# Attention over 16 heads: score tiles issued in groups of three halves instead of four, the value products behind each group, and the work at both ends of the attention reordered

## The chip, the core and the metric

The kernel is one launch on one core of a Trainium2 chip. The core has five engines with in-order instruction queues: TensorE (PE in the profile, its weight loads PEld), VectorE (DVE), ScalarE (ACT), GpSimd (POOL) and SyncE (SP, here only a DMA queue). The metric is the device time of the launch in microseconds; the median of repeated runs is given. SBUF is the on-chip working memory, PSUM the eight banks (128 partitions by 512 fp32 each) that TensorE writes.

## What is computed

The input x has 2 images of 128 channels by 32 by 32 pixels (n = 1024 positions). Each of two blocks normalises x in groups of 4 channels, computes something and adds it to x.

```
x = x + attention(groupnorm(x))        # 8 heads of 16 channels, per image
    q, k, v = W[head] @ t + bias       # (16 x 16) weights per head
    attn = softmax((q^T k) * 16**-0.5, axis=-1)    # 1024 x 1024 per head
    out  = Wp[head] @ (attn @ v) + bp
x = x + convnext(groupnorm(x))         # depthwise 7x7 conv, layernorm over channels,
    h = gelu(y @ w1 + b1)              # 128 -> 512
    y = h @ w2 + b2                    # 512 -> 128
```

There are T = 16 heads in all, heads 0 to 7 for image 0 and 8 to 15 for image 1.

## The kernel before

**Tiles.** A head has NT = 8 tiles of 128 keys; n counts the tiles of all heads (0 to 127). A tile's transposed scores are 128 keys by 1024 queries, made as two halves of 512 columns (`scores_t`, L1040), each in one PSUM bank. h = 2n + c counts these halves. ScalarE takes exp of each half into `pr`, a ring of PR = 4 tiles (L654). `times_v` (L1051) multiplies a whole tile with the values, in four matmuls of 32 output columns, each of which is two instructions. It accumulates a head in one bank.

**The maximum first.** The softmax needs the maximum of each query. For this, the scores are also computed untransposed (`scores`, L993; 2 halves of 512 into one of the two pairs of banks in `sm`) and reduced by VectorE (`maxima`, L766, 128 x 1024), AHEAD = 13 tiles earlier than the exp. `scores(k, 0)` must wait until the maximum of tile k-2 is done, because it reuses its banks. The 8 maxima of a head are split in two parts by GpSimd, turned by TensorE (`turn_max`, L1025), copied by ScalarE (L619) and sent by SP into two more rows of `qs`, so that `scores_t` subtracts them.

**Order of a head.** TensorE's queue is written out by hand: `both_scores(n)` issues for each half one `scores_t` and one `scores` of tile n+13. The two read different 64-row parts of `qs` and `ks` except in the first three tiles of an even head, and can then run side by side. After every second tile come `times_v(n-2)` and `times_v(n-1)`: so the order is four halves, then two value products. The halves, one "turn" use per head (transposed maxima and transposed results, after tile 4) and six "finish" uses (heads 8 and 9 end the attention of image 0; head 14 holds the two group-norm products "mean" and "var" of block 2) take the three banks 4, 5, 7 in rotation. A use waits until the use three before it has been read.

**Before the heads.** TensorE projects q and k of image 0 (L943), runs matmuls on zeros that only keep it active (`keep_busy`, L969), and starts `scores(0)` when the split rows of q and k have been stacked into `qs` and `ks` by DMA (`stack`, L357; SP for q, ScalarE's queue for k). Between the first 13 `scores` tiles stand the value projection of image 0 (`project_v`, L954), both projections of image 1 and its value projection.

**Behind the heads.** In heads 14 and 15 TensorE also runs 56 shifted conv matmuls (L1145, 4 to a unit, 112 instructions) and VectorE twelve conv taps of image 0; then the layernorm of image 0 (`centre_out` L1169, `ln_var`, `ln_turn`, `ln_scale` L1196), the transposes and the projection that end the attention of image 1 (L1240, L1246), the MLP (L1210, L1224), and the same for image 1, whose conv starts after its padded input has been refilled by 32 DMAs (L379).

## Time and profile before

| | us |
|---|---|
| three runs | 312.48, 319.83, 409.74 |
| median of them | 319.83 |
| profiled execution, whole | 313.76 |
| profiled execution, span of the trace | 312.0 |

The execution lasts 1.76 us longer than the span that the trace covers. Within the span PE is busy for 94%, DVE 73%, ACT 57%, POOL 26%. In the page's 40 slices the heads lie in slices 5 to 32. The granted TensorE clock is full but for slice 31, from 234 to 242 us. A busy PE in the page says little, since the ends of matmuls are modelled and overlap: what counts is the distance between the starts of groups, and which wait stands before them. Columns of a timeline row: start, duration, engine, line, operation, output and inputs with their shapes, count of merged instructions, and in brackets the idle time of the engine before and what ended it.

### The profile page before, as it was taken

The page shows a single profiled execution, that of the slowest core. Times are in us where ns is not written, and L with a number is a line of the kernel's source. Part 1 is how long each engine was busy: PE and PEld are TensorE (multiplying, and loading weights), DVE is VectorE, ACT ScalarE, POOL GpSimd, SP SyncE. Part 2 cuts the span into 40 slices and gives each one's busy share as a digit, 9 for nine tenths or more (in the row PEclk, how much of TensorE's full clock was granted, in tenths as well). Part 3 has the DMA queues.
Part 4 walks back from the last instruction along what each step waited for, and adds up shares of the span by engine and source line. Part 5 has one row for each costly group of instructions (what it writes and reads, how often), then busy time and mean ns, then how long its engine had stood idle before and what let it go on. Part 6 is the DMA issues. An engine that isn't in the chain of part 4 may idle for free.

```text
span 312.0 us, 5509 instructions
## 1 busy us (share of the span) xinstructions
PE 291.8 (94%) x2123; PEld 133.2 (43%) x2125; DVE 228.8 (73%) x264; ACT 176.5 (57%) x354; POOL 79.7 (26%) x103
## 2 busy tenths in 40 slices
PE   7999999999999999999999999999989779899895
PEld 2453544454454454454454454444323334323342
DVE  2838868888889979887678989989970228986421
ACT  1304468778778878777778777763173724011321
POOL 7100624323000000000018789983200200101010
PEclk9999999999999999999999999999996999999999
DMA  6275003213203203202113398000000004650001
GB/s 218 36 125 119 1 0 55 35 20 54 43 8 54 47 11 53 52 14 39 29 25 69 103 195 174 8 3 1 2 0 0 2 0 100 159 170 0 2 34 34
DMA packets 8489, 16.32 MB, mean 52 GB/s; under 512 B 2564, under 2 KB 3716, under 8 KB 8464
## 3 DMA queue, kind: packets, MB, share of 16 engines
q1 hardware_dynamic: 7888, 14.96, 22.4%
q10 hardware_dynamic: 576, 1.02, 1.6%
q8 instruction: 17, 0.28, 0.4%
q14 instruction: 8, 0.07, 0.1%
HBM read 4.96 MB, written 1.73 MB: 21 GB/s over the span
## 4 chain that ended last, share of the span: by engine, by line
PE 76%; ACT 8%; DVE 8%; SPq 3%; issue 2%; DMA 2%; POOL 0%; DVEq 0%; ACTq 0%; POOLq 0%
PE ps L1040 19%; PE ps L1051 19%; PE ps L1145 10%; ACT pr L654 7%; PE ps L993 7%; DVE mx L766 4%; PE ps L1210 3%; PE ps L969 3%; SPq L379 3%; PE ps L943 3%; PE ps L1224 2%; PE ps L1169 2%; PE ps L1030 2%; DVE ot L776 2%; PE ps L954 1%
## 5 line engine op out<-in xcount | busy, mean ns | idle before, releaser
L766 DVE TENSOR_REDUCE mx<-ps 128x1 f32<-128x1024 f32 x128 | 151.2, 1220 | 32.9 <-PE ps L993 32.7
L654 ACT ACTIVATE pr<-ps 128x512 f32<-128x512 f32 x256 | 133.2, 602 | 52.9 <-PE ps L1040 52.5
L1040 PE MATMUL ps<-qs,ks 50*128 50x512 f32 x256 | 96.7, 445 | 7.8 <-ACT pr L654 4.9
L993 PE MATMUL ps<-ks,qs 48*128 48x512 f32 x256 | 97.7, 444 | 0.7 <-DVE mx L766 0.7
L1051 PE MATMUL ps<-pr,va 128*32 128x256 f32 x1024 | 69.2, 387 | 0.4 <-ACT pr L654 0.4
L1040 PEld LDWEIGHTS ps<-qs,ks 50*128 50x128 f32 x256 | 43.2, 186 | 61.3 <-ACT pr L654 41.2
L993 PEld LDWEIGHTS ps<-ks,qs 48*128 48x128 f32 x256 | 42.6, 184 | 10.7 <-DVE mx L766 3.5
L1051 PEld LDWEIGHTS ps<-pr,va 128*32 128x32 f32 x1024 | 26.6, 109 | 29.5 <-ACT pr L654 11.5
L804 DVE SCALAR_TENSOR_TENSOR hl<-xpad,w,hl 128x512 f32<-128x512 f32 (+1 forms) x37 | 35.6, 962 | 0.9
L479 POOL CAST mparts<-mx 128x8 fp32r<-128x8 f32 x16 | 3.1, 191 | 127.8 <-DVE mx L766 127.8
L1145 PE MATMUL ps<-xr,wt 128*32 128x512 f32 x272 | 31.1, 594 | 1.0 <-DMA xr<-xpad 1.0
L566 POOL TENSOR_TENSOR hl<-hl 128x1024 f32<-128x1024 f32 x11 | 26.5, 2408 | 0.9
L1210 PE MATMUL ps<-yc,w1g 128*128 128x512 f32 x32 | 15.6, 608 | 2.5 <-DVE yc L848 2.5
L969 PE MATMUL ps<-warm 128*128 128x512 bf16 x57 | 15.7, 409 | 1.6 <-POOL warm L462 1.4
L570 POOL TENSOR_TENSOR rstd<-vareps,power 128x4 f32<-128x4 f32 (+1 forms) x3 | 4.1, 1375 | 47.6 <-DVE vareps L831 47.6
L1145 PEld LDWEIGHTS ps<-xr,wt 128*32 128x32 f32 x272 | 8.0, 109 | 19.0 <-issue 15.9
L711 ACT ACTIVATE pr<-ps,b1s 128x512 f32<-128x512 f32 x8 | 5.5, 688 | 16.8 <-PE ps L1210 16.8
L348 POOL TENSOR_TENSOR gn_rstd<-gn_vareps,power 128x1 f32<-128x1 f32 x4 | 3.8, 942 | 38.1 <-DVE gn_vareps L320 38.1
L563 POOL TENSOR_SCALAR hl<-xpad,w 128x1024 f32<-128x1024 f32 x11 | 12.5, 1140 | 0.7
L609 ACT ACTIVATE va<-ps 128x128 f32<-128x128 f32 x16 | 2.9, 304 | 13.3 <-PE ps L954 13.3
L687 ACT ACTIVATE diag<-inside,w,nshift 128x1024 f32<-128x1024 f32 x2 | 2.5, 1237 | 13.3 <-issue 13.3
L1210 PEld LDWEIGHTS ps<-yc,w1g 128*128 128x128 f32 x32 | 5.6, 189 | 10.1 <-issue 4.7
(104 smaller groups left out, 211.2 us busy)
## 6 DMA issues: line engine op xcount, KB each, us to landing
qs<-hl SPq DMA_DIRECT2D x48, 64.0 KB, 2.4
ks<-hl SPq DMA_DIRECT2D x42, 64.0 KB, 2.4
xr<-xpad SPq DMA_DIRECT2D x16, 95.0 KB, 2.2
xr<-pad_dram SPq DMA_DIRECT2D x4, 361.0 KB, 6.4
xr<-pad_dram SPq DMA_DIRECT2D x4, 304.0 KB, 5.4
xr<-xpad SPq DMA_DIRECT2D x8, 76.0 KB, 2.1
xr<-xpad ACTq DMA_DIRECT2D x8, 76.0 KB, 2.2
xs<-x SPq DMA_DIRECT2D x2, 256.0 KB, 3.0
```

The source lines that it names most:

```text
L379: queue.dma_start(xr[s * CG:(s + 1) * CG, g, lo:hi], xpad[g * CG:(g + 1) * CG, lo + s:hi + s])\
L563: nc.gpsimd.tensor_scalar(image(product), window(0, tap), weight(tap), 0.0, ALU.mult, ALU.add)\
L566: nc.gpsimd.tensor_tensor(acc_pool, acc_pool, product, ALU.add).then_inc(S("pool_tap"), 1)
L654: nc.scalar.activation(pr[:, n % PR, c * HALF:(c + 1) * HALF], bank("half", n, c), ACT.Exp, scale=SCALE).then_inc(exp_done, 1)
L766: nc.vector.tensor_reduce(mx[:, s % 2, i:i + 1], sm[(NT * s + i) % 2], AX.X, ALU.max).then_inc(max_done, 1)
L804: nc.vector.scalar_tensor_tensor(out=sums, in0=window(k, tap), scalar=weight(tap), in1=sums, op0=ALU.mult, op1=ALU.add).then_inc(S("dve_ta ...
L969: nc.tensor.matmul(pv, warm[:, 0:P], warm[:, :], start=True, stop=True)
L993: last = nc.tensor.matmul(sm[k % 2][:, c * HALF:(c + 1) * HALF], qs[rows, cell_of(s) + i * P:cell_of(s) + (i + 1) * P], ks[rows, cell_of(s ...
L1040: nc.tensor.matmul(bank("half", n, c), ks[rows, cell_of(t) + j * P:cell_of(t) + (j + 1) * P], qs[rows, cell_of(t) + c * HALF:cell_of(t) + ...
L1051: last = nc.tensor.matmul(out_v[q * VW:(q + 1) * VW, :], va[:, n * VW:(n + 1) * VW], pr[:, n % PR, 2 * P * q:2 * P * (q + 1)], start=(j == ...
L1145: last = nc.tensor.matmul(conv_out[g * CG:(g + 1) * CG, half * HALF:(half + 1) * HALF], wt[:, g * KS * SPAN + m, :], rows[:, :, 0:SIDE], s ...
L1210: last = nc.tensor.matmul(sm[f % 2][:, cols], w1g[:, f * P:(f + 1) * P], yn[:, b, cols], start=True, stop=True)
```

## The change

- **Groups of three.** `BURST = 3`: TensorE issues three halves, then the value products (`times_v_after`): one when the group ended in the middle of a tile, two when it ended with a tile (and other numbers where a head's first tile is put off, so that it needn't wait for the copy of the head before). The turn and the six finish uses are moved to ends of such groups (`burst_end`).
- **Consequences in other queues.** ScalarE copies a head's result (`copy_u`) after half 3 or 4 of the next head instead of half 1, and makes the conv's border term (`border(0)`) after half 13 of head 14 instead of half 1 of head 15. VectorE normalises a head one tile later.
- **Ahead of the heads.** The value projection of image 0 and one projection of image 1 go in front of `scores(0)`, in the place of 27 keep-busy matmuls (4 are left). The bias product of the MLP (`first_bias`, 4 matmuls) and its addition on VectorE go from head 14 and the end of the conv into the 13 tiles ahead. The stacks of heads 0 and 1 go to SP but for one DMA, and the MLP's weights are loaded before the stacks of heads 2 and 3.
- **Behind the heads.** The transposes and projection of image 1's attention go before the MLP of image 0 (they stood inside it); `turn_u(15)` goes before `ln_scale(0)`, which no longer waits for ScalarE's copy; the other uses of `ln_scale` wait for the product before.

```diff
-TURN_AT = 4
+BURST = 3
 BANKS = (4, 5, 7)
-FINISH = {(HEADS, 6): ("oc", 0), (HEADS + 1, 0): ("oc", 1), (HEADS + 1, 2): ("proj", 0), (HEADS + 1, 6): ("proj", 1),
-          (T - 2, 4): ("mean",), (T - 2, 6): ("var",)}
+
+
+def burst_end(t, x):
+
+    h = 2 * NT * t + x
+    return h + (BURST - 1 - h) % BURST
+
+
+def turn_at(t):
+
+    return burst_end(t, NT)
+
+
+FINISH = {burst_end(HEADS, 13): ("oc", 0), burst_end(HEADS + 1, 1): ("oc", 1), burst_end(HEADS + 1, 5): ("proj", 0),
+          burst_end(HEADS + 1, 13): ("proj", 1), burst_end(T - 2, 10): ("mean",), burst_end(T - 2, 13): ("var",)}
...
             sp.dma_start(bv[:, :], bvrow.rearrange("a p -> p a")).then_inc(S("bv"), 16)
             for n in range(PARTS):
                 stack(sp, 0, 0, n)
-            sp.wait_ge(S("part11", 0), 2)
-            for n in range(PARTS):
-                stack(sp, 0, 1, n)
+            stack(sp, 1, 0, 0, (2,))
+            stack(sp, 1, 0, 1)
+            for i in range(2):
+                for n in range(PARTS):
+                    stack(sp, i, 1, n)
+            sp.dma_start(w1s[:, :], w1).then_inc(S("w12"), 16)
+            sp.dma_start(w2s[:, :, :], w2.rearrange("(f p) c -> p f c", p=P)).then_inc(S("w12"), 16)
             sp.wait_ge(S("minus"), 1)
...
+                for h in range(2 * NT * t, 2 * NT * (t + 1)):
+                    n, c = divmod(h, 2)
+                    a.wait_ge(st_ready, h + 1)
+                    if c == 0 and n >= PR:
+                        a.wait_ge(pv_done, n - PR + 1)
+                    nc.scalar.activation(pr[:, n % PR, c * HALF:(c + 1) * HALF], bank("half", n, c), ACT.Exp,
+                                         scale=SCALE).then_inc(exp_done, 1)
+                    if t and h == 2 * NT * t + (3 if t % BURST else 4):
                         copy_u(t - 1)
-                    if j == TURN_AT and t + 1 < T:
+                    if h == turn_at(t) and t + 1 < T:
                         copy_max(t + 1)
                         if t:
                             copy_turned(t - 1)
...
+            also[2 * NT * (T - 2) + 13] = lambda: border(0)
+            also[2 * NT * (T - 1) + 9] = lambda: ln_square(0)
...
-            keep_busy(9)
+            project_v(0, 0, NT)
+            value_bias()
+            project(1, 0)
...
+            def times_v_after(h):
+
+                n = h // 2
+                if h % 2 == 0:
+                    if n >= PR and (n - PR) % NT == 0:
+                        times_v(n - 4)
+                    if n >= BURST:
+                        times_v(n - 3)
+                else:
+                    if n >= BURST:
+                        times_v(n - 3)
+                    if (n - 2) % NT:
+                        times_v(n - 2)
+
+            def head(t, also=()):
+
+
+                for h in range(2 * NT * t, 2 * NT * (t + 1)):
+                    n, c = divmod(h, 2)
                     scores_t(n, c)
                     if n + AHEAD < NT * T:
                         scores(n + AHEAD, c)
-
-            def head(t, also=()):
-
-
-                for j in range(NT):
-                    n = NT * t + j
-                    both_scores(n)
-                    if j == TURN_AT:
+                    if h % BURST == BURST - 1:
+                        times_v_after(h)
+                    if h == turn_at(t):
                         free("turn", t)
                         if t:
                             turn_u(t - 1)
                         if t + 1 < T:
                             turn_max(t + 1)
-                    if n < 2:
...
-            value_bias()
-            keep_busy(18)
+            keep_busy(4, sm[0][:, 0:HALF])
             for k in range(AHEAD):
                 for c in range(2):
                     scores(k, c)
-                if k == 0:
-                    keep_busy(2)
-                if k in (1, 2):
-                    project_v(0, 4 * (k - 1), 4 * k)
-                if k in (3, 4):
-                    project(1, 0, k - 3, k - 2)
-                if k in (6, 7):
-                    project(1, 1, k - 6, k - 5)
-                if k == NT:
+                if k in (1, 3):
+                    project(1, 1, k // 2, k // 2 + 1)
+                if k == 4:
                     t_.wait_ge(S("copied0"), 1)
-                if k in (NT, NT + 1, NT + 4):
-                    keep_busy(2)
-                if k == NT + 1:
+                if k == 5:
+                    first_bias()
+                if k in (7, 9):
+                    project_v(1, 2 * (k - 7), 2 * (k - 5))
+                if k == 9:
+                    t_.wait_ge(S("b1"), 1)
                     turn_max(0)
-                if k in (NT + 2, NT + 3):
-                    project_v(1, 4 * (k - NT - 2), 4 * (k - NT - 1))
+                if k in (4, 6, 8, 10, 11, 12):
+                    keep_busy(1 + k // 10)
...
             def ln_scale(k):
                 t_.wait_ge(S("diag"), k + 1)
-                t_.wait_ge(*((S("yn"), 2) if k == 2 else (S("yc"), k + 1)))
+                if k:
+                    t_.wait_ge(S("yn"), k)
...
-            head(T - 2, [(5, first_bias)] + [(3 + n * 5 // (2 * units), *quads[n]) for n in range(2 * units)])
+            head(T - 2, [(3 + n * 5 // (2 * units), *quads[n]) for n in range(2 * units)])
             head(T - 1, [(3, centre_out, 0), (5, ln_var, 0), (6, ln_turn, 0)])
-            times_v(NT * T - 2)
-            times_v(NT * T - 1)
+            for n in range(NT * T - 3, NT * T):
+                times_v(n)
+            turn_u(T - 1)
             ln_scale(0)
-            turn_u(T - 1)
-            mlp(0, 0)
             t_.wait_ge(ot_done, T)
             for i in range(NT):
                 last = nc.tensor.transpose(lower[:, i * P:(i + 1) * P], ot[:, i, P:2 * P], ident)
                 if i % (NT // 2) == NT // 2 - 1:
                     last.then_inc(S("ot_T", 1), 1)
-            mlp(0, 1, 0)
             for c, done in enumerate((S("oc", 1), S("oc_low"))):
                 t_.wait_ge(done, 1)
                 nc.tensor.matmul(lower[:, c * HALF:(c + 1) * HALF], vec(C_WP, P), oc[:, 1, c * HALF:(c + 1) * HALF],
                                  start=True, stop=True).then_inc(S("projp", 1), 1)
-            mlp(0, 1, 1)
-            mlp(0, 2)
-            mlp(0, 3)
+            for f in range(FC):
+                mlp(0, f)
```

TensorE in the middle of the heads, before: L1040 is `scores_t`, L993 `scores`, L1051 the value products (four matmuls a tile, so x8 is two tiles).

```order
L1051 MATMUL ps<-pr,va 32x256 x8
L1040 MATMUL ps<-qs,ks 128x512
L993 MATMUL ps<-ks,qs 128x512
L1040 MATMUL ps<-qs,ks 128x512
L993 MATMUL ps<-ks,qs 128x512
L1040 MATMUL ps<-qs,ks 128x512
L993 MATMUL ps<-ks,qs 128x512
L1040 MATMUL ps<-qs,ks 128x512
L993 MATMUL ps<-ks,qs 128x512
L1051 MATMUL ps<-pr,va 32x256 x8
```

The same place of the changed kernel, where the three lines are L1070, L1023 and L1081.

```order
L1081 MATMUL ps<-pr,va 32x256 x8
L1070 MATMUL ps<-qs,ks 128x512
L1023 MATMUL ps<-ks,qs 128x512
L1070 MATMUL ps<-qs,ks 128x512
L1023 MATMUL ps<-ks,qs 128x512
L1070 MATMUL ps<-qs,ks 128x512
L1023 MATMUL ps<-ks,qs 128x512
L1081 MATMUL ps<-pr,va 32x256 x4
```

Six rows of scores instead of eight stand between two groups of value products, which alternate between one tile and two.

TensorE ahead of the heads, before: L969 are the keep-busy matmuls, L963 is `value_bias`, L954 `project_v`, L943 a projection.

```order
L342 MATMUL ps<-gn_spread,w 128x1
L969 MATMUL ps<-warm 128x512 x9
L963 MATMUL ps<-bv,w 128x1
L969 MATMUL ps<-warm 128x512 x18
L993 MATMUL ps<-ks,qs 128x512 x2
L969 MATMUL ps<-warm 128x512 x2
L993 MATMUL ps<-ks,qs 128x512 x2
L954 MATMUL ps<-w,xn 128x128 x4
L993 MATMUL ps<-ks,qs 128x512 x2
L954 MATMUL ps<-w,xn 128x128 x4
```

And in the changed kernel (L975 `project_v`, L964 a projection, L997 keep-busy, L991 `first_bias`).

```order
L975 MATMUL ps<-w,xn 128x128 x8
L984 MATMUL ps<-bv,w 128x1
L964 MATMUL ps<-xn,w 128x512 x2
L997 MATMUL ps<-warm 128x512 x4
L1023 MATMUL ps<-ks,qs 128x512 x4
L964 MATMUL ps<-xn,w 128x512
L1023 MATMUL ps<-ks,qs 128x512 x4
L964 MATMUL ps<-xn,w 128x512
L1023 MATMUL ps<-ks,qs 128x512 x2
L997 MATMUL ps<-warm 128x512
L1023 MATMUL ps<-ks,qs 128x512 x2
L991 MATMUL ps<-w,w1s 128x1 x4
```

The two value projections and one projection no longer stand between `scores` tiles.

TensorE in head 14, before: L1145 are the conv matmuls, L337 and L342 the "mean" and "var" products of block 2.

```order
L1145 MATMUL ps<-xr,wt 32x512 x12
L1040 MATMUL ps<-qs,ks 128x512 x2
L1030 MATMUL ps<-w,u 128x128 x2
L1025 MATMUL ps<-w,mparts 16x128
L337 MATMUL ps<-gn_chan,w 128x1
L1051 MATMUL ps<-pr,va 32x256 x8
L1145 MATMUL ps<-xr,wt 32x512 x12
```

And in the changed kernel, from the same first group of 12 conv matmuls to "mean" (L351).

```order
L1179 MATMUL ps<-xr,wt 32x512 x12
L1070 MATMUL ps<-qs,ks 128x512 x2
L1081 MATMUL ps<-pr,va 32x256 x8
L1060 MATMUL ps<-w,u 128x128 x2
L1055 MATMUL ps<-w,mparts 16x128
L1179 MATMUL ps<-xr,wt 32x512 x12
L1070 MATMUL ps<-qs,ks 128x512 x2
L1179 MATMUL ps<-xr,wt 32x512 x12
L1070 MATMUL ps<-qs,ks 128x512
L1081 MATMUL ps<-pr,va 32x256 x4
L351 MATMUL ps<-gn_chan,w 128x1
```

"mean" now stands behind three groups of 12 conv matmuls instead of one.

## Rows read from the trace of the kernel before

**Rows 1.** The page: busy time by engine, and the group of the maxima.

```profile
PE 291.8 (94%) x2123; PEld 133.2 (43%) x2125; DVE 228.8 (73%) x264; ACT 176.5 (57%) x354; POOL 79.7 (26%) x103
...
L766 DVE TENSOR_REDUCE mx<-ps 128x1 f32<-128x1024 f32 x128 | 151.2, 1220 | 32.9 <-PE ps L993 32.7
```

**Rows 2.** The timeline of all engines, one cycle of two tiles in head 6.

```profile
117.10 1.07 PE L1051 MATMUL ps<-pr,va 128*32 128x256 f32 x16
...
118.10 0.49 PE L1040 MATMUL ps<-qs,ks 50*128 50x512 f32 x1
...
118.63 2.07 ACT L654 ACTIVATE pr<-ps 128x512 f32<-128x512 f32 x4 [0.55 <-PE ps L1040]
...
118.90 2.36 DVE L766 TENSOR_REDUCE mx<-ps 128x1 f32<-128x1024 f32 x2 [0.25 <-PE ps L993]
...
119.28 0.49 PE L1040 MATMUL ps<-qs,ks 50*128 50x512 f32 x1
...
119.72 1.07 PE L1051 MATMUL ps<-pr,va 128*32 128x256 f32 x16
```

**Rows 3.** The same timeline, the cycle of head 6 that holds the turn.

```profile
111.33 1.07 PE L1051 MATMUL ps<-pr,va 128*32 128x256 f32 x16
...
114.49 1.07 PE L1051 MATMUL ps<-pr,va 128*32 128x256 f32 x16
```

**Rows 4.** Timelines of PE, ACT and SP up to the first tile of head 0.

```profile
9.10 1.98 PE L943 MATMUL ps<-xn,w 128*128 128x512 f32 x4 [0.71 <-DVE xn L332]
...
11.84 4.52 SPq L357 DMA_DIRECT2D qs<-hl  x6
...
13.00 2.10 PE L969 MATMUL ps<-warm 128*128 128x512 bf16 x9
...
19.06 0.73 PE L993 MATMUL ps<-ks,qs 48*128 48x512 f32 x2
...
20.91 1.16 PE L954 MATMUL ps<-w,xn 128*128 128x128 f32 x8
...
37.17 1.47 ACT L609 ACTIVATE va<-ps 128x128 f32<-128x128 f32 x8 [3.23 <-PE ps L954]
...
38.74 0.46 PE L1040 MATMUL ps<-qs,ks 50*128 50x512 f32 x1 [0.41 <-issue]
```

**Rows 5.** DVE's timeline: the normalisation of a head, in head 2 and in head 12.

```profile
58.62 0.30 DVE L776 TENSOR_TENSOR ot<-us,rden 128x128 f32<-128x128 f32 x1
...
188.01 1.55 DVE L776 TENSOR_TENSOR ot<-us,rden 128x128 f32<-128x128 f32 x1
```

**Rows 6.** Timelines of PE and DVE in heads 14 and 15.

```profile
208.99 2.78 PE L1145 MATMUL ps<-xr,wt 128*32 128x512 f32 x24
...
212.88 0.38 PE L337 MATMUL ps<-gn_chan,w 128*128 128x1 f32 x2
...
217.30 0.15 DVE L311 COPY gn_mean<-ps 128x1 f32<-128x1 f32 x1
...
225.61 0.21 DVE L326 TENSOR_SCALAR nshift<-gn_mean,gn_rstd 128x1 f32<-128x1 f32 x1
...
231.61 1.28 DVE L817 SCALAR_TENSOR_TENSOR hl<-hl,gn_rstd,diag 128x1024 f32<-128x1024 f32 x1 [2.01 <-ACT diag L687]
...
235.05 3.78 PE L1169 MATMUL ps<-xn,w 128*128 128x512 f32 x4
```

**Rows 7.** Timelines of PE and DVE behind the last value product, and the conv's start.

```profile
246.34 0.64 PE L1051 MATMUL ps<-pr,va 128*32 128x256 f32 x8 [0.37 <-ACT pr L654]
...
248.49 1.96 PE L1196 MATMUL ps<-diag,w 128*128 128x512 f32 x4 [1.51 <-ACT yc L699]
...
252.42 1.98 PE L1210 MATMUL ps<-yc,w1g 128*128 128x512 f32 x4 [1.75 <-DVE yc L848]
...
258.22 1.41 DVE L867 SCALAR_TENSOR_TENSOR xpad<-ps,bout,xs 128x544 f32<-128x544 f32 x2 [2.21 <-PE ps L1246]
...
270.73 10.62 PE ps L1145 x96
```

84 lines of the change are left out of this document (35 added, 49 removed).

## The prediction

> **What bounds the kernel now.** I read the page first, then the timeline of a middle head, then the timelines at both ends, and took each distance from start to start. PE is busy for 94% and the maxima take VectorE 151.2 us, half of the span [rows 1]; neither is the whole answer, because the heads run in cycles in which each engine waits a little. In a cycle of two tiles [rows 2] the reader is to see a closed loop: value products start at 117.10, the first pair of score matmuls 1.00 later, its exp 0.53 after that, the fourth pair 0.65 later (it needs the bank that this exp has read; there are three banks for four halves), and the next products 0.44 later: 1.00 + 0.53 + 0.65 + 0.44 = 2.62, and the products do return after 2.61. VectorE idles 0.25 in it. Once a head the two transposes and the turned maxima stretch the cycle to 3.16 [rows 3], so 0.55 more.
>
> Ahead of the heads, `scores(0)` starts at 19.06 and head 0 at 38.74: 19.7 us for 13 tiles of which VectorE needs 1.13 to 1.23 each [rows 2, 4]; the projections between them, not VectorE, set that pace. Behind the last product, TensorE waits 1.51 for ScalarE's copy and 1.75 for VectorE, and the conv of image 1 starts at 270.73, 12.5 us after the residual that its refill waits for [rows 7].
>
> **Ahead of the heads: -3.5 us.** TensorE is free for the new front at 13.00 [rows 4]. The value projection of image 0 is 16 instructions, twice the x8 group of 1.16 with some overlap, 2.2; the bias product and VectorE's addition behind it about 0.4; the projection 1.9 (1.98 for its x4 group); four keep-busy matmuls 0.9 (2.10 for nine) [rows 4]. That gives 18.4 for `scores(0)`, 0.7 earlier. Its stack must be there: SP begins it at 11.84 and spends 4.52 on six, so the fifth is issued by about 15.6, 2.8 us ahead. Then 13 maxima of 1.13 are 14.7. A tile with a filler of 1.0 to 1.1 behind it costs TensorE about 1.7, more than VectorE's step; there are five of them (two projections, the MLP bias, two value groups), and with two pairs of banks each leaves VectorE some 0.35 without work: 1.8. With 0.3 for the last tile head 0 starts at 18.4 + 14.7 + 1.8 + 0.3 = 35.2. Its other condition, ScalarE's copy of the values, ended last before (37.17 + 1.47, head 0 at 38.74) [rows 4]; the product for it now stands three tiles earlier, so it does not. SP's queue is past the MLP weights and twelve more stack DMAs (18 issues of 0.6 to 0.75, some 12 us) before the turned maxima need it at 32. If it or the copies are late, 2 us are left of the gain; 4.5 if VectorE never waits.
>
> The MLP bias taken out of head 14 I cost at nothing there: VectorE's twelve taps are the longer chain at that place, and hide it.
>
> **In the heads: +2.0 us.** With three halves the three banks suffice, so the 0.65 for the exp leaves the loop. What is late next are the maxima. Call O the group that closes a tile (two products behind it) and E the other. O's first pair completes one tile for VectorE and its third the next, so two maxima run from O + 0.55 for 2.36 [rows 2], till O + 2.91. O's pairs take 0.9 (two steps of 0.24, as 0.73 for two matmuls against 0.49 for one, and 0.44 to the products) and its products 1.00 [rows 2, 4], so E begins at O + 1.9 and could issue its third pair at O + 2.5, but the `scores` in it reuses the banks of the second of these tiles and waits till O + 2.95. Products follow 0.44 later, one of them takes 0.57 (x16 takes 1.07 and x8 0.64 [rows 2, 7], so 0.43 less than 1.00): the next O is at 2.95 + 0.44 + 0.57 = 3.96. Three tiles in 3.96 are 1.32 a tile, against 1.305 now. The loop is closed by VectorE instead of ScalarE and is no shorter: 112 tiles of 14 heads by 0.012 are +1.3. PE's own work in it, 2 x 0.9 + 1.57 = 3.4, and ScalarE's, 6 x 0.52 = 3.1, don't end last. The turn costs its 0.55 as before.
>
> Two smaller terms. While GpSimd runs conv taps, the normalisation takes VectorE 1.55 instead of 0.30 [rows 5]. It does so in three heads; VectorE's slack took most of it up before, and it now stands in the closing chain: 0.4 more each, +1.2 (0 to 3.7, all of it). The finish uses of heads 8 and 9 find their banks earlier: -0.5. Sum +2.0. The bounds: -2 if the third pair waits less than I say, +5 if the extra normalisation counts in full and the first heads, where keep-busy matmuls stand in the groups, lose a us.
>
> **Heads 14 and 15: +2.5 us.** "mean" stood 3.9 behind the first 12 conv matmuls (208.99 to 212.88), and VectorE, which came to it at 217.30, never waited [rows 6]. Now three groups of 12 (2.7 each), five halves, three products and the turn stand ahead of it: 8.1 + 1.8 + 1.4 + 0.5 = 11.8, its result is there at about 12.1, and VectorE comes to it at 8.3: it waits 3.8. Against that the 2.01 that VectorE waits for the border term goes, since ScalarE makes it earlier, and 0.15 for the bias. The conv's result is 1.6 later; TensorE is less behind at that time, so `centre_out` 0.9 later. Two products more than now remain behind `centre_out`: +1.0. And ScalarE: the border term stands behind exp 13 of head 14, issued some 13 us after the first conv group, and needs the shift that VectorE gives at 16.6 now (225.61) and at 20.4 then. Queued behind it are the exps of halves 14 and 15, and for these wait the next head's pairs: TensorE idles about 3.4 us. That is hidden below VectorE's taps, except that the clock, low for `centre_out` already (3.78 for the x4 group [rows 6], where the same form takes 1.98 at full clock [rows 4]), may stay low a little longer: +0.6. Bounds 0 and +6.
>
> **Behind the heads: -3.6 us.** From the start of the last product (246.34) to the conv of image 1 are 24.4 now [rows 7]. TensorE's work in it stays. The 1.51 for the copy shrinks to the 0.5 that the transposes need for u (-1.0); the 1.75 for VectorE's product is filled with the eight transposes and the first half of the projection (-1.75); the refill's residual comes 5 us earlier (253.0 instead of 258.22), so the 1.0 that the conv waits for DMA goes. A tenth is lost between the two halves of the projection: -3.6, -2 to -5. All that follows is TensorE's chain and moves along.
>
> **Sum.** -3.5 + 2.0 + 2.5 - 3.6 = -2.6. The profiled execution took 313.76, so **311.2 us**. That execution is near the lowest of the three runs (312.48); their median, 319.83, is lifted by a run of 409.74, and I forecast on the profiled one.
>
> **A rule against the change.** Start to start, 16 product instructions take 1.00 and 8 take 0.57, so a group of products costs 0.14 however short it is, and ahead of it 0.44 pass from the last pair instead of 0.24: 0.34 a group [rows 2, 4, 7]. There are 8/1.5 = 5.3 groups a head instead of 4, 19 more in 14 heads: 6.4 us of PE, which I take to be within the slack of 3.96 - 3.4. The Trainium skill (TensorEngine Tiling (Array Packing), Key Properties) says that a change of tiling mode, not just of tile, drains TensorE; scores on 64 rows and products on 32 columns are two modes. By that rule every added group is added time, and the sum would be 316.3. The trace agrees that a switch has a price, and puts it beside VectorE's chain.
>
> **Rivals.** (1) The groups pay: if the third pair's wait mostly vanishes, three tiles cost what VectorE needs with small gaps, 3 x 1.18 = 3.5 to 3.8 instead of 3.92, some 37 times: -4 to -15 for the heads instead of +2. For it: the fourth pair's wait for an exp is plainly in the rows and plainly removed. Against it: two pairs of `sm` banks are all that `scores` has. The turn and the switches stay, so I take -6 from this span: without the heads' term the sum is 309.2, with it 303. (2) Slower, by the drains: TensorE becomes the bound of the loop, which it does when six pairs, three products and two switches pass 3.96; all 6.4 counts instead of 1.3: 316.3. Against it: 3.4 by the rows. (3) Head 14: the low clock lasts from ScalarE's stall through both heads, and some 9 us of matmuls take twice as long where they are on the path, 4 more: 315. (4) The front is not earlier, since a stack DMA or the turned maxima land late: 314.5.
>
> **Chances.** Forecast 0.44 (307.5 to 313.5), (1) 0.30, (2) 0.12, (3) 0.08, (4) 0.06. The range, 303 to 316.5, leaves out the lower half of (1) and a little above. A difference of 2% is 6.3 us, about what a measurement of this kernel can tell. Faster than 307.5: (1) and a little of the forecast's edge, 0.35. Slower than 320.0: the upper ends of (2) and (3), 0.05. Within: 0.60.
>
> **What would show it.** Head 0 near 35.2. In a middle head the products 3.95 apart every second time, `scores` of the third pair waiting for a maximum and no wait for an exp; a period near 3.6 speaks for (1), and PE without any idle time there for (2). VectorE idle 3 to 4 us before the mean copy, and ScalarE about 8 us in front of the border term. From the last product to the conv of image 1 some 20.8. The forecast is wrong if the heads gain several us, or if the front gains under 2.

## The result, and the profile after

The changed kernel takes **328.84 us** (median of four, 326.19 to 330.26) where the kernel before took 316.15 beside it (312.29 to 409.74). The ratio is 1.052, with an interval of 1.040 to 1.063: **slower by 5%**, and outside the range. "Same" had the best chance, "slower" 0.05. The profiled execution took 326.19 us.

Two numbers tell the executions of this case apart, and every result below is read with both. The first is the time. The second is how long TensorE was granted its lower level, 1.2 of 2.4 GHz, which is 2 x (1 - mean granted clock) x span; I call it the **low time**. Two executions of one kernel show what it costs: ends_only (below) took 302.63 us without any and 318.66 with 38.0, so 0.42 us for each us at the lower level; front_only went from 308.40 to 322.77 with 33.5 more of it, 0.43. A time less 0.42 x low time is called the time **at full clock**. Ratios leave out the executions that took over 1.5% more than the fastest of their kernel, and since these are the subject here I give all times beside them.

First the page of the kernel after: span, busy times, granted clock in 40 slices, and the maxima.

```profile
span 324.4 us, 5462 instructions
PE 306.4 (94%) x2101; PEld 134.1 (41%) x2103; DVE 227.6 (70%) x264; ACT 179.4 (55%) x354; POOL 79.2 (24%) x103
PEclk9999999999999999679999959966995799999999
L786 DVE TENSOR_REDUCE mx<-ps 128x1 f32<-128x1024 f32 x128 | 151.8, 1220 | 43.4 <-PE ps L1023 43.0
```

The same clock row of the kernel before:

```profile
PEclk9999999999999999999999999999996999999999
```

TensorE has 22 instructions fewer than in [rows 1] and is busy 14.6 us longer, and is still at 94%. The share of busy time says nothing here; the clock row does. Four dips stand where one stood. The windows of the kernel after give them in numbers (stretch, length, then busy time of PE, its weight loads, DVE, ACT and POOL, the granted clock, DMA):

```profile
120.00:140.00 20.00, 19.50 (x147) 9.22 (x145) 14.74 (x15) 13.86 (x28) 0.78 (x4) 0.80 0.12 21
140.00:160.00 20.00, 19.73 (x152) 8.49 (x144) 13.20 (x16) 14.73 (x31) 0.39 (x2) 0.94 0.22 38
...
180.00:200.00 20.00, 18.99 (x131) 8.32 (x129) 15.21 (x16) 13.47 (x29) 17.76 (x13) 0.83 0.67 138
200.00:220.00 20.00, 18.96 (x146) 8.97 (x149) 15.73 (x16) 13.10 (x27) 13.63 (x12) 0.85 0.11 21
...
240.00:260.00 20.00, 16.53 (x89) 6.03 (x81) 9.94 (x13) 10.12 (x18) 1.59 (x1) 0.74 0.00 1
```

With the stretches' own bounds it is 132.1 to 142.3, 186.7 to 193.5, 214.0 to 224.2 and 244.7 to 254.9, and the last 1.2 us of the span: 39 us. The kernel before has one, 233.1 to 239.9, and the last 0.5.

What a fall looks like, in two-us windows and in PE's timeline of the kernel after:

```profile
130.00:132.00 2.00, 2.00 (x18) 1.13 (x14) 1.31 (x2) 1.38 (x4) 0.00 (x0) 1.00 0.56 98
132.00:134.00 2.00, 2.00 (x17) 0.85 (x18) 1.44 (x2) 0.66 (x2) 0.00 (x0) 0.53 0.00 0
```

```profile
131.37 0.39 PE L1070 MATMUL ps<-qs,ks 50*128 50x512 f32 x1
...
131.91 1.80 PE L1081 MATMUL ps<-pr,va 128*32 128x256 f32 x16
...
134.67 0.62 PE L1070 MATMUL ps<-qs,ks 50*128 50x512 f32 x1
```

TensorE is shown without a stop in the two us ahead of this fall. The same products took 1.07 in [rows 2] and take 1.80, the same score matmul goes from 0.39 to 0.62. Up to here the kernel was ahead (head 8 began at 128.7, before at 129.7); head 9 begins at 146.1, before at 142.0.

Now the rows that answer to the prediction's steps. The loop of three tiles at full clock, in head 0:

```profile
46.64 0.50 PE L1023 MATMUL ps<-ks,qs 48*128 48x512 f32 x1
...
47.07 0.64 PE L1081 MATMUL ps<-pr,va 128*32 128x256 f32 x8
...
50.62 0.18 PEld L1023 LDWEIGHTS ps<-ks,qs 48*128 48x128 f32 x1 [0.56 <-DVE mx L786]
...
51.05 0.64 PE L1081 MATMUL ps<-pr,va 128*32 128x256 f32 x8
```

The single product of group E returns after 3.98 us (forecast 3.96), and the third pair's `scores` waits for a maximum, as forecast against [rows 2]. Then heads 14 and 15, on DVE, ACT and PE, in order:

```profile
234.24 0.16 DVE L325 COPY gn_mean<-ps 128x1 f32<-128x1 f32 x1 [3.77 <-PE ps L351]
...
242.81 1.24 ACT L700 ACTIVATE diag<-inside,w,nshift 128x1024 f32<-128x1024 f32 x1 [7.54 <-DVE nshift L340]
...
244.58 1.70 PE L1070 MATMUL ps<-qs,ks 50*128 50x512 f32 x3 [3.41 <-ACT pr L667]
```

VectorE waits 3.77 for the mean (3.8 said), ScalarE 7.54 for the shift (about 8), TensorE 3.41 for the exps behind it (3.4). And both ends:

```profile
35.73 0.49 PE L1070 MATMUL ps<-qs,ks 50*128 50x512 f32 x1
...
261.89 1.50 PE L1081 MATMUL ps<-pr,va 128*32 128x256 f32 x24
263.89 0.44 PE L1060 MATMUL ps<-w,u 128*128 128x128 f32 x2 [0.50 <-ACT u L658]
...
283.27 1.07 PE L1179 MATMUL ps<-xr,wt 128*32 128x512 f32 x8
```

Head 0 begins at 35.73 (35.2 said; 38.74 in [rows 4]). Of the three products from 261.89 the last begins at 262.77, and the conv of image 1 follows 20.5 later (20.8 said; 24.4 in [rows 7]). So each structural step is in the trace with its size, and the kernel is still 15 us slower than the sum.

### The profile page after: what moved, and what is told of

The parts are those of the page before. It is cut to its first block, busy times and chain, and to the rows that moved or that the text cites. A ratio compares the mean times of both kernels' runs of the same rounds, so it can differ in the third digit from the quotient of the medians.

```text
span 324.4 us, 5462 instructions
## 1 busy us (share of the span) xinstructions
PE 306.4 (94%) x2101; PEld 134.1 (41%) x2103; DVE 227.6 (70%) x264; ACT 179.4 (55%) x354; POOL 79.2 (24%) x103
## 4 chain that ended last, share of the span: by engine, by line
PE 76%; DVE 17%; ACT 2%; issue 2%; DMA 2%; SPq 0%; POOL 0%; DVEq 0%; ACTq 0%; POOLq 0%
PE ps L1070 19%; PE ps L1081 18%; DVE mx L786 11%; PE ps L1023 10%; PE ps L1179 9%; PE ps L1237 4%; PE ps L1251 4%; DVE hl L824 2%; PE ps L1060 2%; PE ps L1195 2%; DVE ot L796 2%; DMA w<-wpack 2%; PE ps L997 1%; ACT pr L667 1%; PE ps L964 1%
## 5 line engine op out<-in xcount | busy, mean ns | idle before, releaser
L667 ACT ACTIVATE pr<-ps 128x512 f32<-128x512 f32 x256 | 136.4, 599 | 52.8 <-PE ps L1070 45.1
L1070 PE MATMUL ps<-qs,ks 50*128 50x512 f32 x256 | 101.9, 466 | 5.5 <-ACT pr L667 4.3
L1023 PE MATMUL ps<-ks,qs 48*128 48x512 f32 x256 | 101.5, 461 | 4.4 <-DVE mx L786 3.9
L1081 PE MATMUL ps<-pr,va 128*32 128x256 f32 x1024 | 78.0, 411 | 0.0
L1070 PEld LDWEIGHTS ps<-qs,ks 50*128 50x128 f32 x256 | 45.4, 197 | 60.1 <-ACT pr L667 35.5
L1023 PEld LDWEIGHTS ps<-ks,qs 48*128 48x128 f32 x256 | 44.1, 192 | 19.5 <-DVE mx L786 15.9
L1081 PEld LDWEIGHTS ps<-pr,va 128*32 128x32 f32 x1024 | 25.5, 112 | 34.7 <-issue 16.2
L1179 PE MATMUL ps<-xr,wt 128*32 128x512 f32 x272 | 33.3, 632 | 0.0
L732 ACT ACTIVATE pr<-ps,b1s 128x512 f32<-128x512 f32 x8 | 5.5, 688 | 16.8 <-PE ps L1237 16.8
L997 PE MATMUL ps<-warm 128*128 128x512 bf16 x35 | 11.8, 456 | 1.6 <-POOL warm L478 1.4
L658 ACT ACTIVATE u<-ps 128x256 f32<-128x256 f32 x16 | 6.1, 384 | 9.9 <-PE ps L1081 9.8
L635 ACT ACTIVATE mrows<-ps 16x128 fp32r<-16x128 f32 x16 | 4.3, 266 | 11.8 <-PE ps L1055 11.6
```

What stands on the lines that cost most here:

```text
L667: nc.scalar.activation(pr[:, n % PR, c * HALF:(c + 1) * HALF], bank("half", n, c), ACT.Exp, scale=SCALE).then_inc(exp_done, 1)
L997: nc.tensor.matmul(where, warm[:, 0:P], warm[:, :], start=True, stop=True)
L1023: last = nc.tensor.matmul(sm[k % 2][:, c * HALF:(c + 1) * HALF], qs[rows, cell_of(s) + i * P:cell_of(s) + (i + 1) * P], ks[rows, cell_of(s ...
L1070: nc.tensor.matmul(bank("half", n, c), ks[rows, cell_of(t) + j * P:cell_of(t) + (j + 1) * P], qs[rows, cell_of(t) + c * HALF:cell_of(t) + ...
L1081: last = nc.tensor.matmul(out_v[q * VW:(q + 1) * VW, :], va[:, n * VW:(n + 1) * VW], pr[:, n % PR, 2 * P * q:2 * P * (q + 1)], start=(j == ...
L1179: last = nc.tensor.matmul(conv_out[g * CG:(g + 1) * CG, half * HALF:(half + 1) * HALF], wt[:, g * KS * SPAN + m, :], rows[:, :, 0:SIDE], s ...
```

## The experiments

The theory (**clock**): at full clock the change is worth about what was forecast, and what is lost are stretches at 1.2 GHz that some part of it brings. The rival (**structure**): a wait that the shown rows miss costs the 15 us, and the low stretches are an effect beside it. The change falls into three parts that can be made apart: the **groups** of three in the heads, the **front** (all that moves ahead of head 0) and the **back** (all behind the last product).

### The parts alone

`ends_only` has front and back, and groups of four as before; `groups_only` has only the groups. A diff marked "short" shows the lines that name its part and leaves out the others that go with them.

```diff
# ends_only against after (short)
-BURST = 3
+TURN_AT = 4
...
-                    if h % BURST == BURST - 1:
-                        times_v_after(h)
+                    if j % 2 == 0 and n:
+                        times_v(n - 2)
+                        times_v(n - 1)
# groups_only against before (short)
-TURN_AT = 4
+BURST = 3
...
-                    if j % 2 == 0 and n:
-                        times_v(n - 2)
-                        times_v(n - 1)
+                    if h % BURST == BURST - 1:
+                        times_v_after(h)
```

> The changed kernel with the order of the heads as before: groups of four halves, the finish uses, the border term and VectorE's normalisation where they were; the front, the MLP bias and the part behind the last product are those of the change. Theory A (the groups of three let TensorE's clock fall to 1.2 GHz inside the heads): head 0 at 35.7, no more low-clock time than before (6.8 us within the span before), the last product to the conv in 20.5 instead of 24.4, so 3.0 + 3.9 less than before: 306 to 308. Theory B (the fall comes from the front or from the chip, not from the groups): low clock in the heads here too, 315 to 325. Theory C (the groups cost their time in the loop and in the late mean, the clock only follows): as A, 306 to 308.

> The kernel before with the groups of three and what they move (finish uses, border term, copy of a head's result, normalisation), but its own front, MLP bias in head 14 and its own part behind the last product. Theory A: low clock for 25 to 40 us of the heads, as in the changed kernel, and 3.0 + 3.9 more than it: 330 to 338. Theory B: full clock in the heads, 313 to 319. Theory C: 330 to 338 as A.

ends_only: 302.63, 314.35, 316.04, 318.66 us with low times of 0, 27.5, 31.4, 38.0. groups_only: 321.02, 325.21, 329.39, 332.27 with 7.0, 16.8, 27.5, 30.4; its two fastest give a ratio of 1.027 (1.011 to 1.043). So front and back gain 8 us at full clock, of which one execution of four got all; groups alone lose 7.6 at full clock and have low stretches on top. In the profile of groups_only one of them, 65.3 to 75.5, lies in head 2.

`front_only` and `back_only` part the two ends; back_only is all the lines shown, front_only all of the change ahead of head 0:

```diff
# front_only against before (short)
-            value_bias()
-            keep_busy(18)
+            keep_busy(4, sm[0][:, 0:HALF])
...
+                if k == 5:
+                    first_bias()
# back_only against before
-            gelus(0, 0, 1)
...
-            ln_scale(0)
             turn_u(T - 1)
-            mlp(0, 0)
+            ln_scale(0)
...
-            mlp(0, 1, 0)
...
-            mlp(0, 1, 1)
-            mlp(0, 2)
-            mlp(0, 3)
+            for f in range(FC):
+                mlp(0, f)
```

> The kernel before with the change's front alone (projections and values ahead of the scores, stacks on SP, MLP bias there). Full-clock time 3.5 to 4.5 below that of before (310.6), 306 to 307. If the 27 keep-busy matmuls that it drops were what kept the clock up later, low time 20 to 50 us in each run and a median of 315 to 325; if not, as before, 4 to 24 us low, 309 to 316.

> The kernel before with the change's order behind the last product alone (transposes and projection ahead of the MLP, turn ahead of the scale). Full-clock time 3.9 below before, 306.7; low time as before, 4 to 24 us: 308 to 317. It can't act on the heads, which are all ahead of it; if its low time differs from that of before, low time varies by itself between chips or programs.

front_only: 308.40 once with 4.3 low, and 322.43, 322.77, 322.82 with 38. back_only: 307.17 twice without any, 308.36 and 308.72 with 4; ratio **0.979 (0.974 to 0.985)**, clear of 1, though not of a difference of 2%. Its page:

```profile
span 305.3 us, 5508 instructions
PEclk9999999999999999999999999999999999999999
```

Each end is worth about 4 us at full clock, and the front loses three times that in three of four executions. `groups_back` closes the table: groups and back, the front as before.

```diff
# groups_back against after (short)
-            keep_busy(4, sm[0][:, 0:HALF])
+            value_bias()
+            keep_busy(18)
```

> Groups of three and the back of the change, the front as before. If the parts add up at full clock: groups alone about 318, less 3.9 of the back, so 314 us with no stretch at 1.2 GHz, and with 7 to 30 us of such stretches inside the heads (as groups_only showed) 317 to 327. If the falls inside the heads came from the change's front and not from the groups, the clock would be full in the heads and the time 310 to 314.

316.30 to 327.29 (median 322.56), low time 6.9 to 31.2; its two fastest give a ratio of 1.012 (1.008 to 1.016).

| kernel | median us | mean low time | at full clock | executions |
|---|---|---|---|---|
| before | 313 to 316 | 9 | 310.8 | 57 |
| back | 307.8 | 2 | 307.0 | 4 |
| front | 322.6 | 30 | 306.7 | 4 |
| front + back | 315.2 | 24 | 302.7 | 4 |
| groups | 327.3 | 20 | 318.4 | 4 |
| groups + back | 322.6 | 20 | 313.6 | 6 |
| all (the change) | 328.8 | 47 | 308.7 | 4 |

The last column is the mean of time less 0.42 x low time. For the change it leans on the 0.42 most, since its four executions have 39 us of low time or more: with 0.35 to 0.46 it would be 312 to 307. (`after_bias_old`, below, stands for the same structure with 6.8 us, and gives 309.4.) At full clock the parts add up: back -3.8, -4.0 and -4.8 by the three pairs that differ in it alone, front -4.1, -4.3 and -4.9, groups +7.6, +6.6 and +6.0. The change is -2.1 (+1 to -4 by the bounds of its row), the forecast was -2.6. The low time is 38 us more, 16 us of time. That is the loss.

### Does work for TensorE keep the clock up?

`fill2` puts two short matmuls on unused columns of the products' bank into every second group of the changed kernel (unlike what its expectation says, they do change the sums of the value products, so only its time is of use); `ends_fill` puts one 48-row matmul per two tiles into ends_only, `after_fill` two into every second group of the change.

```diff
# after_fill against after (ends_fill: the same function, one matmul, at c == 1 and n % 2 == 0)
+            def fill(k, c, n):
+                rows = slice(rows_of(k // NT), rows_of(k // NT) + STACK)
+                for _ in range(n):
+                    nc.tensor.matmul(sm[k % 2][:, c * HALF:(c + 1) * HALF], warm[rows, 0:P], warm[rows, :],
+                                     start=True, stop=True)
...
+                    if h % (2 * BURST) == 1 and n >= PR and n + AHEAD < NT * T:
+                        fill(n + AHEAD, c, 2)
# fill2 against after
+                for _ in range(n):
+                    nc.tensor.matmul(pv[:, 2 * P:HALF], warm[rows, 0:P], warm[rows, 0:2 * P], start=True, stop=True,
+                                     skip_group_check=True)
...
+                    if h % (2 * BURST) == 2 and latest[0] % NT != NT - 1:
+                        fill(t, 2)
```

> The changed kernel with two small matmuls on zeros (64 rows, 256 columns, bf16) added in front of the scores matmul that waits for a maximum, in 33 of the 42 groups that have such a wait; they write unused columns and change no result. Theory A: TensorE's waits are filled, the clock stays at 2.4 GHz in most of the heads, granted clock of the run 0.97 or more, and the time falls to 312 to 318 in spite of the added work. Theory C (the loop and the late mean cost the time): no change or up to 3 slower than the change, 326 to 331.

> E1 (the change's two ends, groups of four as before) with one matmul on zeros (48 rows, 512 columns, bf16, 0.22 us) in each group, ahead of the fourth pair, whose wait for an exp is 0.22; it writes the scores half that the next matmul overwrites, and needs no wait of its own. So far every run fits a full-clock time plus 0.42 times its time at 1.2 GHz (E1: 302.7 and 0 to 38 us low). Theory A (the clock falls because the cycle leaves TensorE unfilled): low time per run under 5 us in most runs, median 303 to 306. Theory D (the falls don't depend on what stands in TensorE's waits): 0 to 38 us low as before, median 312 to 318.

> The changed kernel with two such matmuls (0.43 us) in every second group of three, ahead of the scores matmul of its second pair; the group's later wait for a maximum, 0.4 to 0.5, takes them up. Theory A: low time falls from 39 to 51 us to under 15, median 309 to 315 (full-clock time 308.7). Theory D: low time stays, 325 to 332.

fill2: 320.93, 327.57, 332.99, 335.45 with 24 to 55 low. after_fill: 321.18 and 322.60 with 15, 332.55, 333.25, 333.50 with 41, 351.14 with 82; its two fastest give a ratio of 1.024 (1.016 to 1.032), and it is at 315 to 316 at full clock. ends_fill: 307.63 and 308.05 with 7 and 8, four at 319.4 to 319.8 with 34 to 35; 304.9 at full clock. Fillers in the heads cost 2 to 7 us and end no low stretch reliably. As a remedy this fell.

### The late mean

`mean_early` takes the mean of image 1 in the changed kernel three halves earlier and the variance three, so that the border term, and the exps that are queued behind it, need not wait as long; `groups_back_mean` does so in groups_back.

```diff
-          burst_end(HEADS + 1, 13): ("proj", 1), burst_end(T - 2, 10): ("mean",), burst_end(T - 2, 13): ("var",)}
+          burst_end(HEADS + 1, 13): ("proj", 1), burst_end(T - 2, 9): ("mean",), burst_end(T - 2, 11): ("var",)}
```

> The changed kernel with the finish use mean at half 9 of head 14 (with the turn) instead of 12, and var at half 12 instead of 15. Theory A and C agree on the place: VectorE's wait of 3.77 for the mean goes, the shift comes 3 to 4 earlier, ScalarE's 7.5 in front of the border term becomes under 4, TensorE's idle 3.4 in head 15 goes: 3 to 5 less than the change where the clock is the same, 321 to 327. If the late mean costs nothing because the clock sets head 14: under 1 less.

> Groups of three with the earlier mean, the front as before, the back of the change. At full clock 313.4 (e11) less the 3.5 of the earlier mean: 310. If groups of three bring falls inside the heads whatever the front: 3 to 30 us at 1.2 GHz, 311 to 323 us. If the stall at the border term was what brought them: 310 to 313 in all.

mean_early: 320.62, 320.83, 321.40, 332.57 with 34 to 61 low; its three fastest give a ratio of 1.021 (1.009 to 1.032), 306.2 at full clock, so -2.5. But its profile has a stretch of 31 us at 1.2 GHz ahead of head 0, of which more below. groups_back_mean: 309.55, 309.67 and 309.86 without any low time, 312.68, 314.65 and one of 323.42; its four fastest give a ratio of **0.989 (0.984 to 0.995)**, and it is at 310.2 at full clock. Beside groups_back this is the cleanest pair. First groups_back, then groups_back_mean:

```profile
225.72 0.16 DVE L323 COPY gn_mean<-ps 128x1 f32<-128x1 f32 x1 [4.69 <-PE ps L349]
...
234.29 1.24 ACT L698 ACTIVATE diag<-inside,w,nshift 128x1024 f32<-128x1024 f32 x1 [7.54 <-DVE nshift L338]
...
236.06 1.21 PE L1058 MATMUL ps<-qs,ks 50*128 50x512 f32 x3 [3.41 <-ACT pr L665]
```

```profile
221.00 0.15 DVE L323 COPY gn_mean<-ps 128x1 f32<-128x1 f32 x1
...
229.56 1.24 ACT L698 ACTIVATE diag<-inside,w,nshift 128x1024 f32<-128x1024 f32 x1 [2.63 <-DVE nshift L338]
```

The mean is there when VectorE comes to it, ScalarE waits 2.63 instead of 7.54, and TensorE's stop of 3.41 is gone from the timeline. That is worth 3.4 at full clock, and the mean low time falls from 20 to 7. In groups_back the clock falls at 237.6, 1.5 us behind that stop, and in the changed kernel at 244.7, right behind its own. So the late mean makes a low stretch at that place likelier, besides its own wait: groups_back has 6.9 us or more in all six executions, groups_back_mean none in three of six. It is not the only way there, since the kernel before has its one stretch in head 15 too, with the mean in time.

What is left of the groups, compared without any difference of clock (both profiles are at 1.00 till the last us): head starts of groups_back_mean less those of back_only are -0.3 at head 0, +1.1 at 4, +1.7 at 8, +2.8 at 12, +2.4 at 14, and the span is 2.3 longer. The whole times say the same without any correction: 309.55, 309.67 and 309.86 against 307.17 twice, all of them without low time, +2.5. The loop is no shorter, and a head is 0.26 us longer over the first twelve. The windows of back_only and then of groups_back_mean:

```profile
20.00:120.00 100.00, 96.50 (x761) 48.21 (x764) 84.06 (x81) 70.32 (x153) 19.68 (x45) 1.00 0.23 41
```

```profile
20.00:120.00 100.00, 97.25 (x743) 46.58 (x742) 81.57 (x80) 69.98 (x151) 19.63 (x45) 1.00 0.22 39
```

VectorE, which closes the loop, does 2.5 us less work in these 100, while TensorE is shown busier.

### The early stretch: bias product, fillers, order or wait?

In the profiles of mean_early and ends_fill the clock falls at 26.4 and 26.8, among the first score matmuls, and stays low for 27 to 31 us. The MLP bias product stands just ahead of that. Two kernels part it from the fillers that the front has fewer of: `ends_bias_old` returns the product to head 14, `ends_busy` adds fillers between the first scores.

```diff
# ends_bias_old against ends_only (short)
-                if k == 5:
-                    first_bias()
...
-                if k in (4, 6, 8, 10, 11, 12):
+                if k in (4, 5, 6, 8, 10, 11, 12):
...
+            head(T - 2, [(5, first_bias)] + [(3 + n * 5 // (2 * units), *quads[n]) for n in range(2 * units)])
# ends_busy against ends_only
-                if k in (4, 6, 8, 10, 11, 12):
-                    keep_busy(1 + k // 10)
+                if k in (4, 5, 6, 8, 10, 11, 12):
+                    keep_busy(2)
```

> Groups of four, front and back of the change, but the MLP bias product (eight one-column matmuls) back in head 14 and one filler matmul in its place. Theory A (the chain of one-column matmuls sets off the long stretch at 1.2 GHz early in the kernel that front_only and ends_only showed in three executions of four): no stretch of 27 us or more before the heads in any execution, 302 to 306 us. Theory B (the 25 filler matmuls fewer ahead of and among the first scores set it off): as ends_only, 302.6 or 314 to 319 us, most executions the latter, with head 0 at 40 us or later where it falls.

> Groups of four, front and back of the change, bias product in the front, but two filler matmuls after each of seven of the first thirteen scores groups instead of one or two. Theory B (too few filler matmuls among the first scores): no early stretch at 1.2 GHz, 303 to 306 us (fillers that wait for nothing may cost up to 1.5 us). Theory A (bias product): the early stretch stays in most executions, 314 to 320 us.

ends_busy: 304.94 and 306.76, then four of 317.8 to 325.3 with 34 to 54 low: more fillers there do not help. ends_bias_old: 304.67, 304.92, 305.41, 305.41 with 4 low, 323.85 with 51; the first four give a ratio of 0.974 (0.971 to 0.977); a sixth took 1417 us (last section). It read like the answer, and the repetition took it back:

> e9 once more, for a profile of an ordinary execution: 304.7 to 305.5 us, head 0 at about 35 us, no stretch at 1.2 GHz in heads 0 to 13. One execution of e9 took over a thousand us; if that belongs to the kernel, it comes again here.

The same kernel again: 305.91, and 320.05, 320.37, 323.86 with 38 to 51 low. Four of its nine ordinary executions fall. In the profiled one (320.05), in one-us windows:

```profile
25.00:26.00 1.00, 0.99 (x4) 0.39 (x3) 1.00 (x2) 0.61 (x1) 0.00 (x0) 1.00 0.63 90
26.00:27.00 1.00, 0.92 (x4) 0.42 (x3) 1.00 (x2) 0.00 (x0) 0.00 (x0) 0.89 0.71 107
```

The clock falls at 26.8 with no bias product in the front. The product is not needed for the fall.

The opposite test, `back_bias`, puts the product alone into back_only's front, after the sixth scores:

```diff
# back_bias against back_only (short)
+                if k == 4:
+                    t_.wait_ge(S("copied0"), 1)
+                if k == 5:
+                    first_bias()
...
                 if k == NT + 1:
+                    t_.wait_ge(S("b1"), 1)
                     turn_max(0)
```

> Groups of four, the front as before, the back of the change, and of the change's front only the MLP bias product (after the sixth scores group, weights loaded earlier). back_only ran at 307.2 to 308.7 us with 0 to 4 us at 1.2 GHz. If the product by itself sets off the early stretch: 27 us or more at 1.2 GHz in some executions and 318 us or more in those. If it needs the few filler matmuls of the new front as well: 306 to 309 us in all.

All six executions fall: 325.55 to 334.53 with 39 to 61 low; the five fastest give a ratio of 1.044 (1.041 to 1.047). But the edit added something that I had not counted, a wait for a copy that in this front comes late. PE's timeline and windows:

```profile
28.98 1.22 PE L1002 MATMUL ps<-ks,qs 48*128 48x512 f32 x2 [2.21 <-ACT hl L637]
```

```profile
27.00:28.00 1.00, 0.00 (x0) 0.00 (x0) 0.00 (x0) 1.00 (x2) 0.00 (x0) 1.00 0.43 78
28.00:29.00 1.00, 0.03 (x1) 0.03 (x1) 0.00 (x0) 0.92 (x1) 0.00 (x0) 0.76 0.03 4
```

TensorE stopped at 26.8 and the clock fell at about 28.5, ahead of the product at 30.1. So in this profile it is the wait that the fall follows, not the product. `back_nofill` makes such a wait with nothing else, by taking 14 of the 18 fillers ahead of the first scores:

```diff
-            keep_busy(18)
+            keep_busy(4)
```

> back_only with 4 filler matmuls ahead of the first scores instead of 18. Nothing else moves, so TensorE either starts its scores up to 3.0 us earlier or waits there for the stacked rows. If an idle stretch of 2 us or more in the front sets off the early fall (as the 2.21 us wait in front of the bias product did in back_bias, whose clock fell 2 us after it began, in all six executions): 27 us or more at 1.2 GHz in most executions and 318 us or more. If not: 304 to 308 us.

```profile
18.62 1.22 PE L992 MATMUL ps<-ks,qs 48*128 48x512 f32 x2 [2.67 <-DMA ks<-hl]
```

```profile
16.00:17.00 1.00, 0.00 (x0) 0.00 (x0) 0.00 (x0) 0.00 (x0) 0.00 (x0) 1.00 0.91 201
17.00:18.00 1.00, 0.00 (x0) 0.00 (x0) 0.00 (x0) 0.00 (x0) 0.00 (x0) 0.97 0.92 123
18.00:19.00 1.00, 0.38 (x1) 0.38 (x2) 0.00 (x0) 0.00 (x0) 0.00 (x0) 0.50 0.72 111
```

314.80 with 21 low, and five executions of 327.79 to 332.54 with 47 to 60. The scores start only 0.6 earlier than in back_only (18.62 against 19.19), since they wait for their stacked rows; the fillers were hiding little but a stop of 2.67 us, and the clock falls 2.0 us after it begins. It stays at 1.2 GHz for 47.7 us. (back_only has 4 us or less in all four.) A stop of this kind in the front is enough: with it, the two kernels have at least 39 us of low time in eleven of twelve executions and 21 in the other; the kernel before and back_only, with the old front and no such stop, have at most 24 in 61.

It is not necessary. `ends_warm` gives ends_bias_old its 18 fillers back:

```diff
-            keep_busy(4, sm[0][:, 0:HALF])
+            keep_busy(18, sm[0][:, 0:HALF])
```

> ends_bias_old with 18 filler matmuls of full rows ahead of the first scores instead of 4 (as the kernel before has them); scores start about 3.0 us later (14 x 0.216). If these fillers are what keeps the clock up in the kernel before: no early stretch at 1.2 GHz in any execution, 305.5 to 308 us, about the time of back_only. If it is the order among the first scores (the V projections of image 0 gone ahead of them, 48-row scores with one filler behind): the early stretch in about half the executions, 306 or 320 to 327 us.

306.75 without low time, 309.29, 310.21, 314.74 with 21, and 327.54, 328.35 with 51; the three fastest give a ratio of 0.984 (0.977 to 0.990), and it is at 306.8 at full clock. In its profile, where no wait above 0.35 stands ahead:

```profile
29.00:30.00 1.00, 0.92 (x4) 0.39 (x3) 1.00 (x2) 0.00 (x0) 0.00 (x0) 1.00 0.70 119
30.00:31.00 1.00, 1.00 (x5) 0.72 (x4) 1.00 (x2) 0.00 (x0) 0.00 (x0) 0.52 0.59 103
```

The scores begin 3.0 later than in ends_bias_old (21.47 against 18.49) and the fall comes 3.2 later (30.0 against 26.8), in both within the fourth of four tiles of 48-row scores that have one filler between them. In these two profiles the fall goes with that run of work. The front before has projections of 128 rows between most of those scores; the new one has spent its value projections ahead of them. The early stretches of the profiles last 27 us or more. Over all kernels with the new front and groups of four, 20 of 35 executions have that much low time; with the old front (before and back_only) none of 61, the highest being 24. These executions come from four chips, and the odds on one chip were not separated from the rest: ends_bias_old fell once in five on one and three times in four on another, while the kernel before beside them had 20 us or more in 2 of 7, 2 of 11, 0 of 11, 3 of 17 and 2 of 11, and 27 in none. The order is what differs; which property of it counts was not isolated.

### The change without the bias product

`after_bias_old` is the change with the edit of ends_bias_old, and the second kernel adds the edit of mean_early:

```diff
# after_bias_old against after (short)
-            head(T - 2, [(3 + n * 5 // (2 * units), *quads[n]) for n in range(2 * units)])
+            head(T - 2, [(5, first_bias)] + [(3 + n * 5 // (2 * units), *quads[n]) for n in range(2 * units)])
# the second kernel, besides
-          burst_end(HEADS + 1, 13): ("proj", 1), burst_end(T - 2, 10): ("mean",), burst_end(T - 2, 13): ("var",)}
+          burst_end(HEADS + 1, 13): ("proj", 1), burst_end(T - 2, 9): ("mean",), burst_end(T - 2, 11): ("var",)}
```

> The whole change, but the MLP bias product back in head 14 with one filler matmul in its place. Its full-clock time should be that of the changed kernel, about 309. If the groups of three bring the falls inside the heads by themselves: 20 to 50 us at 1.2 GHz and 317 to 330 us, near the changed kernel. If the bias product in the front brings them all (as it brought the early stretch with groups of four): few low stretches and 309 to 313 us.

> As e12, and mean and variance of image 1 two to three halves earlier in head 14, which gave 3 us at full clock and took away the stretch at 1.2 GHz behind the border term. If groups bring the falls: about 306 at full clock and 7 to 30 us at 1.2 GHz, so 309 to 318 us. If the bias product brings them all: 306 to 309 us.

The whole change with the product in head 14, twelve executions: 312.28 with 6.8 low up to 331.05 with 48, median 322.8; the three fastest give a ratio of 1.003 (0.999 to 1.007). At full clock 309.6: this kernel's best executions give the change's time at full clock nearly without extrapolation, 309.4 from 312.28. Its profile has a low stretch in heads 13 and 14 (203.8 to 214.0) and one behind the border term's stop. With the earlier mean too: 305.16 and 305.74 without any low time (by these two the ratio is 0.976, 0.973 to 0.979), then 311.19, 320.80, 322.42, 327.30; 305.4 at full clock. So the falls inside the heads neither need the product nor come with every execution of the groups. Of the nine profiles of kernels with groups of three, six have a stretch at 1.2 GHz that begins within heads 0 to 13 (two of the six are the ones with fillers in the heads); of the ten ordinary profiles with groups of four, none.

## Why the prediction was wrong

**Right: what the pieces do.** Front: -3.0 in the profile and -4.1 to -4.9 at full clock by pairs (said -3.5). Back: -3.8 to -4.8 (said -3.6). The loop is closed by the maxima at 3.98 us for three tiles (said 3.96), not shortened. All three waits of head 14 are within 0.5 us of the forecast. At full clock the change is -2.1 (said -2.6), and that they agree so closely is in part luck: the last column of the table is uncertain by 2 us or more there, both ends gained more than said and the groups cost more.

**Undersized: the groups.** Said +2.0 for the heads and +2.5 for heads 14 and 15. Measured at full clock the groups are +6.0 to +7.6. In the pair with the back, +6.6, the earlier mean gives back 3.4, so the late one, for which heads 14 and 15 had their 2.5, was 0.9 more than said, and 3.2 stay, 1.2 more than the 2.0. The executions without any low time give 2.5 for this rest instead of 3.2, and the late mean then 4.1, so the late mean is the term that was mis-sized most. (The working of the heads has a slip as well: 1.32 less 1.305 is 0.015, and 112 times that is 1.7 and not 1.3, which makes its term 2.4.) What makes the other pairs differ by a us I can't place. Rival (1), that groups pay, is refuted by the unmoved loop; rival (2), the drains as the bound of the loop, by the wait of `scores` on VectorE that is still there. Rival (4) did not happen.

**The failed step: the clock.** The sum carries it as "the clock, low for `centre_out` already ..., may stay low a little longer: +0.6", and rival (3) adds 4 us for heads 14 and 15, with a chance of 0.08. Unwritten, and on which all other terms rest, is that TensorE keeps 2.4 GHz everywhere else because it did so in one execution of the kernel before. The runs show a kernel in which the order of work moves the odds of low stretches in three places: ahead of head 0 (new front with groups of four: 20 of 35 executions), inside the heads (groups of three: six of nine profiles), and in head 14 behind the stop that the late mean makes. The changed kernel has all three risks and 47 us of low time on average against 9; 38 x 0.42 is 16 us. The stop in head 14 was in my working, with its 3.4 us; I priced it as hidden, and its price was what comes after it.

**Structure against clock.** The rival theory of a missed wait is refuted by the executions of single kernels, the same instructions in the same order, whose times go with their low time (ends_only 302.6 or 318.7, the change without its bias product 312.3 or 331.0), and by the parts adding up once the clock is taken out.

**Open.** What in a run of uninterrupted work lets the clock fall; how much of the odds is the chip's; whether the bias product adds to it (low time of the change is at least 39 in all four executions, without the product 7 to 48 in twelve); why an execution falls and the next of the same kernel does not.

**The version to keep** is back_only: 307.8 us, ratio 0.979 (0.974 to 0.985), none of its four executions above 309. ends_only and the change with earlier mean and the product in head 14 have faster best executions (302.6 and 305.2) and medians of 315 to 316.

## What to carry to other kernels

Read the granted clock of several executions before summing stages: a us at the lower level cost about 0.42 us in this kernel (0.35 to 0.46 by the executions of each version, 0.30 by the changed kernel's own four, which lie close together), so a schedule that exposes it can lose more than it saves in waits. Filler matmuls that seem to cost time ahead of a wait are to be judged by what follows the wait, and a stop of TensorE that a change adds, of 2.2 to 3.4 us here, should be removed first, even where it is hidden. Repeat a remedy for a matter of chance before believing it: four clean executions of ends_bias_old of five became five of nine.
